# Graph attention on one core: segment maxima by scans over 32 steps at once

## The chip, the cores and the metric

One of the eight cores of a Trainium2 chip runs one program. The metric is the device time in microseconds (us); the kernel before takes 11579.1 us, the median of three runs.

## The reference

Four graph layers over 12,500 nodes of 128 features, each followed by a residual and a layer norm. The edges, 200,000 of them, are sorted by their target `dst`. Layer 0 averages neighbours, layer 1 mixes the 16 neighbours of a ring, layer 2 is graph attention, layer 3 is two graph convolutions. The change is in layer 2:

```
hs = h[src]
a  = hs @ Ws.T + h[dst] @ Wd.T + emb_rel[etype] @ Wr.T
e  = leaky_relu((a @ attn_fc2_w.T)[:, 0], 0.01)        # one logit an edge
m  = segment_max(e, dst);  w = exp(e - m[dst])
denom = segment_sum(w, dst);  alpha = w / denom[dst]
agg = segment_sum(alpha[:, None] * hs, dst)
agg = where(deg > 0, agg, h);  out = agg + h @ loop_weight
```

## The kernel before

Nodes stand in 98 tiles of 128. The sorted edges are cut into 1660 steps (`STEPS`) of up to 128 edges, so that the targets of one step lie in one node tile; an edge is a partition, a step a column of `src_idx` and `dst_local` (the target's place in its tile). Three layers walk over the steps in turn. In the attention stage every step j does this:

- GpSimd gathers 128 rows of 132 words (128 features, a one, the source's part of the logit, two coefficients) from `attention_rows` in HBM by an indirect DMA (L1987) into one of 28 row slots; a slot is free when the product of step j-28 is done (`a_summed`) and its group of 7 steps is drawn (`a_coefs`).
- VectorE builds a one-hot [edge, node] in bf16 (L2052, `edges_hot`); TensorE turns it (L2095), ScalarE copies it out of PSUM (L2120, `nodes_hot`), and TensorE multiplies it by three bf16 pieces of the target's scores (L2087). Every 7 steps `draw_vector` (L2002 to L2011) makes the logits.
- VectorE masks the logits into a [edge, node] matrix (L2043), TensorE turns it (L2080), VectorE takes the maximum over the edges for each node (L2037) and then the minimum with the node's running negative maximum (L2033). ScalarE makes the factor for the old sum (L2113), keeps the maximum (L2116) and takes the exponentials of the whole matrix (L2108). TensorE turns the weights back (L2073), ScalarE copies them (L2104), TensorE multiplies by the gathered rows (L2069, two passes in float32), and VectorE scales the accumulator and adds (L2025). Each `added` waits for the one before.

Steps are staggered by hand: every engine walks over the same list of moments (`steps_due`, 28 hops) and does, in a fixed order, what is due for different steps. Two matmuls a step (`keep_warm`, L2059) have no reader. Each VectorE, ScalarE and TensorE part that addresses a node tile reads its column from registers, loaded eight steps at a time.

Before the stage: `attention_gpsimd` begins when the dense product of layer 1 is done. SyncE reloads step data and then loads `loop_rows` (6.4 MB, L1923) into `x_all` for the layer's end. After it: `finish3` walks over the 98 tiles on VectorE (divide by the denominator, add the loop row L2167, add own rows of nodes with no edge L2161, statistics and norm); SyncE loads own rows through an 8-slot ring (L2176). Then the convolution stage follows.

## Time and profile before

| | |
|---|---|
| median of 3 runs (lowest, highest) | 11579.1 us (11574.55, 11604.76) |
| span of the profiled execution, first to last instruction | 9485.5 us |
| time of the profiled execution outside its span | not reported by the profile |
| median less span | 2093.6 us |
| instructions in the trace | 179289 |
| mean granted TensorE clock (1.0 is full speed) | 0.865 |

Of an engine the profile gives busy time (the union of its instructions) and idle time ahead of each group of instructions, with the instruction of another engine whose semaphore ended it ("<- PE banks L2069"); "issue" is a wait for which the profile shows no releaser. Instructions of one engine overlap at their ends, so that the mean durations of a step's instructions add up to more than the busy time.

### The profile page before, as it was taken

To read this page: it belongs to the slowest core of one execution; us is meant where nothing else is said; L and a number is where in the kernel's file an instruction comes from. 1 tells how busy PE (TensorE), PEld (TensorE's weight loads), DVE (VectorE), ACT (ScalarE), POOL (GpSimd) and SP (SyncE) were. 2 spreads that over 40 slices of the span, in tenths; PEclk is the share of its full clock that TensorE was granted. 3 is DMA by queue.
4 is the path that set the end of the run, shared out by engine and by line. 5 is a ranking of instruction groups with operands and counts; after the bars stand their busy time and mean duration, and the time that the engine had idled before them with its cause. 6 is when DMAs were issued, how large, how long until landed. Compare 5 with 4: busy or idle time off the path is not lost.

```text
span 9485.5 us, 179289 instructions
## 1 busy us (share of the span) xinstructions
PE 7300.6 (77%) x42403; PEld 5513.2 (58%) x42403; DVE 7417.6 (78%) x24801; ACT 6576.3 (69%) x18731; POOL 6416.0 (68%) x6972
## 2 busy tenths in 40 slices
PE   4444444555689999999989999788888888838887
PEld 3333444444467777788878787555555555525555
DVE  7766666666788999566667777788888888899899
ACT  6777777777877777111178866577777777758885
POOL 0377777777347777777677777666666666639894
PEclk8555555555799999999999999999999999979997
DMA  3222222222477777888877752322222222210001
GB/s 55 50 53 53 53 53 52 53 52 53 125 257 258 254 260 257 317 327 318 292 267 257 254 191 67 84 51 50 50 51 50 50 51 50 50 36 1 1 2 28
DMA packets 499507, 1146.68 MB, mean 121 GB/s; under 512 B 149534, under 2 KB 352994, under 8 KB 478894
## 3 DMA queue, kind: packets, MB, share of 16 engines
q0 software_dynamic: 212688, 491.92, 19.3%
q10 hardware_dynamic: 21888, 497.76, 13.5%
q1 hardware_dynamic: 263902, 145.55, 5.7%
q8 instruction: 369, 6.05, 0.3%
q14 instruction: 660, 5.41, 0.2%
HBM read 888.41 MB, written 252.74 MB: 120 GB/s over the span
## 4 chain that ended last, share of the span: by engine, by line
PE 27%; DVE 27%; issue 17%; ACT 14%; POOL 7%; DVEq 4%; DMA 2%; SPq 1%; ACTq 0%; POOLq 0%
PE banks L1423 17%; POOL step_data L1765 7%; ACT banks L1185 3%; DVE step_small L2037 3%; DVE keys L2043 3%; PE banks L1049 2%; PE banks L1409 2%; DVE keys L1109 2%; ACT onehot L1038 2%; DVE gather_ring L2243 2%; DVE keys L1118 2%; ACT onehot L1036 2%; DVEq L1065 2%; DVE arena L2253 2%; DVE arena L2025 2%
## 5 line engine op out<-in xcount | busy, mean ns | idle before, releaser
L1024 POOL DMA_INDIRECT gather_ring<-mean_rows,step_data x1660 | 1597.4, 962 | 744.2 <-issue 322.4
L1049 PE MATMUL banks<-gather_ring,onehot 128*128 128x130 f32 x3320 | 950.9, 449 | 1127.4 <-DVE arena L1082 949.0
L1423 PE MATMUL banks<-arena 128*128 128x384 bf16 x8232 | 1549.0, 327 | 30.5 <-DMA arena<-split_out 26.5
L1049 PEld LDWEIGHTS banks<-gather_ring,onehot 128*128 128x128 f32 x3320 | 792.5, 301 | 1280.1 <-issue 1047.2
L1423 PE MATMUL banks<-arena,keys 128*128 128x384 bf16 x8134 | 1529.0, 327 | 3.9 <-DMA arena<-split_im 3.9
L1423 PEld LDWEIGHTS banks<-arena 128*128 128x128 bf16 x8232 | 1133.8, 138 | 263.2 <-issue 31.2
L1423 PEld LDWEIGHTS banks<-arena,keys 128*128 128x128 bf16 x8134 | 1119.8, 138 | 232.9 <-issue 5.0
L1765 POOL DMA_INDIRECT step_data<-next_rows,window_idx x992 | 945.3, 953 | 347.8 <-issue 300.2
L1456 POOL DMA_INDIRECT step_data<-hidden,window_idx x924 | 897.7, 972 | 323.2 <-issue 267.0
L1987 POOL DMA_INDIRECT gather_ring<-attention_rows,step_data x834 | 788.3, 945 | 392.9 <-PE banks L2069 218.5
L1987 POOL DMA_INDIRECT keys<-attention_rows,step_data x826 | 779.5, 944 | 367.7 <-PE banks L2069 254.8
L2059 PE MATMUL banks<-iota_quad,ident_half 128*128 128x256 bf16 x3320 | 913.5, 275 | 104.4 <-DVE arena L2025 86.1
L1036 ACT ACTIVATE onehot<-iota_row,step_data 128x128 f32<-128x128 f32 x1660 | 644.4, 388 | 436.4 <-PE banks L1049 410.7
L2226 POOL TENSOR_SCALAR onehot<-iota_row,step_data,window_idx 128x128 f32<-128x128 f32 x996 | 777.6, 792 | 84.6 <-PE banks L2291 63.3
L1082 DVE TENSOR_TENSOR arena<-arena,banks 128x130 f32 x1660 | 482.0, 290 | 402.7 <-DVE arena L1082 229.2
L2025 DVE SCALAR_TENSOR_TENSOR arena<-arena,step_small,banks 128x129 f32 x1660 | 581.8, 351 | 226.3 <-ACT step_small L2113 84.3
L2113 ACT ACTIVATE step_small<-arena,step_small 128x1 f32 x1660 | 489.3, 295 | 350.2 <-DVE step_small L2033 321.3
L1456 POOL DMA_INDIRECT gather_ring<-hidden,window_idx x612 | 591.9, 967 | 207.0 <-issue 177.5
L1038 ACT ACTIVATE onehot<-onehot,ones 128x128 f32<-128x128 f32 x1660 | 666.4, 401 | 53.8
L1415 ACT ACTIVATE arena<-banks 128x392 bf16<-128x392 f32 x1088 | 519.9, 501 | 196.0 <-PE banks L1409 143.3
L2080 PE MATMUL banks<-ident,keys 128*128 128x128 f32 x1660 | 539.6, 325 | 144.4 <-DVE keys L2043 53.5
L1415 ACT ACTIVATE keys<-banks 128x392 bf16<-128x392 f32 x1056 | 506.7, 498 | 199.9 <-PE banks L1409 147.0
(324 smaller groups left out, 19507.1 us busy)
## 6 DMA issues: line engine op xcount, KB each, us to landing
keys<-count_rows ACTq DMA_DIRECT2D x48, 3136.0 KB
arena<-count_rows ACTq DMA_DIRECT2D x48, 3136.0 KB
count_rows<-arena ACTq DMA_DIRECT2D x25, 3136.0 KB
count_rows<-keys ACTq DMA_DIRECT2D x25, 3136.0 KB
gather_ring<-mean_rows,step_data POOLq DMA_INDIRECT x1660
step_data<-next_rows,window_idx POOLq DMA_INDIRECT x992
step_data<-hidden,window_idx POOLq DMA_INDIRECT x924
gather_ring<-attention_rows,step_data POOLq DMA_INDIRECT x834
```

Of the source, the lines that this page charges most:

```text
L1024: e.indirect_dma_start(ring_at(rings.slot(name, i), SUM_COLS, SUMS - 1), None, rows, bass.IndirectOffsetOnAxis(src_idx[:, i:i + 1], 0), bo ...
L1036: e.activation(h, iota_row[:, :], ACT.Abs, bias=dst_local[:, j:j + 1], scale=-1.0).then_inc(hot_made)
L1038: e.activation(h, h, ACT.Relu, bias=ones[:, 0:1], scale=-1.0).then_inc(hot_made)
L1049: e.matmul(pass_bank[i % N_SUM_BANKS][:, 0:SUMS], onehot[:, i % STEP_SLOTS, :], ring_at(rings.slot(name, i), SUM_COLS, SUMS), start=True, ...
L1415: e.activation(counts[t % 2][:, 4 * g:4 * g + 4, :], count_bank[b % len(count_bank)][:, 0:GROUP_COLS].rearrange("p (q h) -> p q h", q=4), ...
L1423: m = e.matmul(pass_bank[n % 2][:, 0:SPLIT_COLS], counts[t % 2][:, :, h], split[:, h, :], start=(h == 0), stop=(h == NODE_TILES - 1))
L1456: e.indirect_dma_start(first_rows(i)[:, a, :], None, hidden1, bass.IndirectOffsetOnAxis(gather_idx[:, at:at + 1], 0), bounds_check=None).t ...
L1765: e.indirect_dma_start(batch_rows[:, i % BATCH_SLOTS, r, :], None, next_rows, bass.IndirectOffsetOnAxis(gather_idx[:, at:at + 1], 0), boun ...
L1987: e.indirect_dma_start(attention_row(j), None, attention_rows, bass.IndirectOffsetOnAxis(src_idx[:, j:j + 1], 0), bounds_check=None).then_inc(
L2025: e.scalar_tensor_tensor(part, part, step_small[:, s, 3:4], step_sums(j), ALU.mult, ALU.add).then_inc(a_added)
L2059: e.matmul(bank[:, 0:WARM_COLS], ident_half[:, :], warm_row, start=True, stop=True)
L2226: e.tensor_scalar(onehot[:, p % CONV_HOTS, :], iota_row[:, :], dst_local[:, j:j + 1], edge_norm[:, j:j + 1], ALU.is_equal, ALU.mult).then_ ...
```

## The change

A step no longer holds a masked matrix and per-node maxima. Since edges are sorted by target, a node's edges are a contiguous run, within a step or over several. For a span of 32 steps at once (52 spans, the last of 28 steps) the logits [128 edges, 32 steps] are turned to [32 steps, 128 edges]; a forward and a backward scan that add -2^100 at each change of target and take maxima (`local_vector`), a scan over the 32 ends (`cross_vector`, on one partition) and two scans with the carried-in maxima (`final_vector`) give each edge its segment's maximum. One Exp makes all 32 x 128 weights; one node a span, that which began in the span before, has its sum rescaled. A step then keeps: one weighted one-hot (float32, VectorE), one product, one addition. The bf16 one-hots of the logits are made four steps in one instruction, turned by plain matmuls, and copied four at once. `keep_warm` is gone. The rows ring has 96 slots, in the arena, where `x_all` was filled with loop rows; `finish3` now loads loop rows tile by tile, beside the own rows. `flags_vector` makes the flags of continued segments from a new load (`last_target`) before the first step. Span work of the coming span is placed at fixed distances (`left`) before the end of the running span.

```diff
-HOT_SLOTS = 2 * STEP_SLOTS
+SPAN, SPAN_SLOTS, HOT_BATCH = 32, 3, 4
+SPANS = -(-STEPS // SPAN)
+SPAN_SIZES = [min(SPAN, STEPS - g * SPAN) for g in range(SPANS)]
...
-        for s in range(FEW_SLOTS):
-            e.wait_ge(loop_stored[s], 16 * len(range(s, NODE_TILES, FEW_SLOTS)))
-        e.dma_start(x_all.rearrange("p (t d) -> p t d", d=D),
-                    loop_rows.rearrange("(t p) d -> p t d", p=P)).then_inc(x_loaded, 16)
+        e.dma_start(last_target, step_rows[P - 1:P, STEP_COLS:2 * STEP_COLS]).then_inc(steps_back, 16)
...
+    def moments():
+        for g in range(-1, SPANS):
+            first, n = (0, SPAN) if g < 0 else span_of(g)
+            for i in range(n):
+                yield g, g + 1 if g + 1 < SPANS else None, i, i - n, first + i if g >= 0 else None
+    def batch_due(p, i, hop):
+        b, odd = divmod(i - hop, 2)
+        return b if p is not None and not odd and 0 <= b < SPAN_SIZES[p] // HOT_BATCH else None
...
-                e.wait_ge(a_summed, j - ATTENTION_SLOTS + 1)
-                e.wait_ge(a_coefs, 2 * ((j - ATTENTION_SLOTS) // DRAWN + 1))
-            e.indirect_dma_start(attention_row(j), None, attention_rows,
+            if j >= ROW_SLOTS:
+                if j % SPAN == 0:
+                    e.wait_ge(a_coefs, 2 * ((j - ROW_SLOTS) // SPAN + 1))
+                e.wait_ge(a_summed, j - ROW_SLOTS + 1)
+            e.indirect_dma_start(row_ring[:, j % ROW_SLOTS, :], None, attention_rows,
                                  bass.IndirectOffsetOnAxis(src_idx[:, j:j + 1], 0),
-                                 bounds_check=None).then_inc(
-                rings.landed("attention", j // DRAWN)[0], 16)
...
+    def flags_vector(e):
...
+        e.wait_ge(steps_back, 64)
+        e.tensor_copy(target_half[:, :], dst_local).then_inc(a_flags)
...
+        e.tensor_tensor(broken_whole, first, last_target, ALU.not_equal).then_inc(a_flags)
+        e.wait_ge(a_flags, 3)
+        e.tensor_tensor(flag_room[:, 1:], flag_room[:, 1:], last_target[:, :-1], ALU.subtract).then_inc(a_flags)
...
+    def logits_vector(e, p):
...
+        rows = row_ring[:, first % ROW_SLOTS:first % ROW_SLOTS + n, :]
+        l, done, cols = logit[:, p % 2, 0:n], DRAW_STEPS * p, slice(first, first + n)
+        e.wait_ge(a_score, batches_before(p + 1))
+        if p >= 2:
+            e.wait_ge(a_tensor, SCALES * (p - 2) + LOGITS)
+        e.tensor_reduce(l, span_scores(p, n), AX.X, ALU.add).then_inc(a_logit)
+        e.wait_ge(*rings.landed("attention", p))
+        e.tensor_copy(edge_norm[:, cols], rows[:, :, D + 3]).then_inc(a_coefs)
...
+    def local_vector(e, p):
+        n = SPAN_SIZES[p]
+        e.wait_ge(a_scalar, SCALE_KEPT * p + RESET)
+        e.wait_ge(a_tensor, SCALES * p + LOGITS)
+        e.tensor_tensor_scan(forward[0:n, 0:P], reset[0:n, 0:P], span_logits[0:n, :], -MASK, ALU.add,
+                             ALU.max).then_inc(a_vector)
+        e.tensor_tensor_scan(backward[0:n, P - 1::-1], reset[0:n, P:0:-1], span_logits[0:n, ::-1], -MASK, ALU.add,
+                             ALU.max).then_inc(a_vector)
+    def cross_vector(e, p):
+        first, n = span_of(p)
+        heads = head_rows[n < SPAN]
+        e.wait_ge(a_tensor, SCALES * p + TAILS)
...
+    def final_vector(e, p):
+        first, n = span_of(p)
+        done = ROW * p + CROSSED
+        e.wait_ge(a_tensor, SCALES * p + CARRIES)
+        e.tensor_copy(carry_kept[0:n, :], span_carry[0:n, :]).then_inc(a_vector)
...
+        e.tensor_tensor_scan(carried[0:n, 0:P], reset[0:n, 0:P], span_logits[0:n, :], carry_kept[0:n, 0:1], ALU.add,
+                             ALU.max).then_inc(a_vector)
+        e.wait_ge(a_vector, done + 2)
+        e.tensor_tensor_scan(highest[0:n, P - 1::-1], reset[0:n, P:0:-1], carried[0:n, P - 1::-1],
+                             carry_kept[0:n, 1:2], ALU.add, ALU.max).then_inc(a_vector)
+        e.wait_ge(a_vector, done + 3)
+        if p:
+            e.wait_ge(a_tensor, SCALES * (p - 1) + BACK)
...
+    def weighted_vector(e, j):
+        g = j // SPAN
+        if j >= STEP_SLOTS:
+            e.wait_ge(a_summed, j - STEP_SLOTS + 1)
+        e.wait_ge(a_scalar, SCALE_KEPT * g + WEIGHT)
+        e.tensor_scalar(onehot[:, j % STEP_SLOTS, :], iota_half[:, :], dst_local[:, j:j + 1],
+                        weight[:, g % SPAN_SLOTS, j % SPAN:j % SPAN + 1], ALU.is_equal, ALU.mult).then_inc(a_weighted)
+    def added_vector(e, j, late_regs):
+        g, i = divmod(j, SPAN)
+        if j:
+            e.wait_ge(a_added, j)
+        if i == 0:
+            part, = late_regs.parts(e, j, (0, D + 1))
+            e.wait_ge(a_scalar, SCALE_KEPT * g + SCALE_KEPT)
+            e.scalar_tensor_tensor(part, part, scale_kept, part, ALU.mult, ALU.add).then_inc(a_scaled)
+            e.wait_ge(a_scaled, g + 1)
+        part, = late_regs.parts(e, j, (0, D + 1))
+        e.wait_ge(a_summed, j + 1)
+        e.tensor_tensor(part, part, sum_bank[j % SUM_SLOTS], ALU.add).then_inc(a_added)
...
+        flags_vector(e)
+        for g, p, i, left, j in moments():
+            if (b := batch_due(p, i, 0)) is not None:
+                k, at = batches_before(p) + b, p * SPAN + b * HOT_BATCH
+                if k >= HOT_BUFS:
+                    e.wait_ge(a_turned, k - HOT_BUFS + 1)
+                e.tensor_tensor(
+                    edges_hot[:, k % HOT_BUFS, :, :],
+                    target_half[:, at:at + HOT_BATCH].rearrange("p (o c) -> p o c", o=1).to_broadcast([P, P, HOT_BATCH]),
+                    iota_quad[:, :, :], ALU.is_equal).then_inc(a_hot)
+            if p is not None:
+                if left == -14:
+                    e.wait_ge(a_scalar, SCALE_KEPT * p + TARGETS_KEPT)
+                    if p:
+                        e.wait_ge(a_scalar, SCALE_KEPT * (p - 1) + RESET)
+                    n = SPAN_SIZES[p]
+                    e.tensor_tensor(change[0:n, 0:P - 1], targets[0:n, 0:P - 1], targets[0:n, 1:P],
+                                    ALU.not_equal).then_inc(a_vector)
+                if left == -12:
+                    logits_vector(e, p)
+                if left == -10:
+                    local_vector(e, p)
+                if left == -8:
+                    cross_vector(e, p)
+                if left == -6:
+                    final_vector(e, p)
+                if left == -4:
+                    rescale_vector(e, p)
+                if left >= -WEIGHT_AHEAD:
+                    weighted_vector(e, p * SPAN + WEIGHT_AHEAD + left)
+            if j is not None:
+                if left < -WEIGHT_AHEAD:
+                    weighted_vector(e, j + WEIGHT_AHEAD)
                 if j:
-                    e.wait_ge(a_added, j)
-                e.scalar_tensor_tensor(part, part, step_small[:, s, 3:4], step_sums(j), ALU.mult,
-                                       ALU.add).then_inc(a_added)
...
+        for g, p, i, left, j in moments():
+            if (b := batch_due(p, i, 3)) is not None:
+                k, n = batches_before(p) + b, SPAN_SIZES[p]
+                e.wait_ge(a_nodes, k + 1)
+                if p >= 2 and b == 0:
+                    e.wait_ge(a_logit, DRAW_STEPS * (p - 2) + 1)
...
+                    m = e.matmul(span_scores(p, n)[:, step, :], nodes_hot[:, k % HOT_BUFS, c * P:(c + 1) * P], parts,
+                                 start=True, stop=True)
+                m.then_inc(a_score)
+            if (b := batch_due(p, i, 1)) is not None:
+                k = batches_before(p) + b
+                if k >= TURN_BUFS:
...
+                first, n = span_of(p)
+                if left == -16:
+                    if p:
+                        e.wait_ge(a_scalar, SCALE_KEPT * (p - 1) + TARGETS_KEPT)
+                    e.transpose(span_targets[0:n, :], dst_local[:, first:first + n], ident[:, :]).then_inc(a_tensor)
...
+                    e.transpose(span_scale, rescale_row, ident[0:1, 0:1]).then_inc(a_tensor)
+            if j is not None:
+                if j >= SUM_SLOTS:
+                    e.wait_ge(a_added, j - SUM_SLOTS + 1)
+                e.wait_ge(a_weighted, j + 1)
+                e.matmul(sum_bank[j % SUM_SLOTS], onehot[:, j % STEP_SLOTS, :], row_ring[:, j % ROW_SLOTS, 0:D + 1],
+                         start=True, stop=True).then_inc(a_summed)
...
+        for g, p, i, left, j in moments():
+            if (b := batch_due(p, i, 2)) is not None:
+                k = batches_before(p) + b
+                e.wait_ge(a_turned, k + 1)
+                if k >= HOT_BUFS:
+                    e.wait_ge(a_score, k - HOT_BUFS + 1)
+                e.activation(nodes_hot[:, k % HOT_BUFS, :], turn_bank[k % TURN_BUFS], ACT.Copy).then_inc(a_nodes)
+            if p is not None:
...
+                if left == -4:
+                    if p >= SPAN_SLOTS:
+                        e.wait_ge(a_weighted, (p - SPAN_SLOTS + 1) * SPAN)
+                    e.wait_ge(a_tensor, SCALES * p + BACK)
+                    e.activation(weight[:, p % SPAN_SLOTS, 0:n], span_back[:, 0:n], ACT.Exp).then_inc(a_scalar)
...
+            e.dma_start(loop_many[:, t % 8, :], loop_rows[tile_rows(t), :]).then_inc(piece_stored[t % 8], 16)
...
-        e.wait_ge(a_kept, STEPS)
```

## Rows read from the trace of the kernel before

**Rows 1.** Windows: length, busy (count) of PE, PEld, DVE, ACT, POOL, clock, DMA share, GB/s.

```profile
374.00:2482.00 2108.00, 1006.74 (x3832) 853.73 (x3832) 1393.35 (x2344) 1588.12 (x3637) 1592.84 (x1659) 0.56 0.25 56
2482.00:6022.00 3540.00, 3362.54 (x19959) 2706.89 (x19959) 2719.56 (x7730) 2063.90 (x4013) 2435.40 (x2530) 0.98 0.70 248
6032.00:8371.00 2339.00, 1902.57 (x13280) 1234.26 (x13280) 1997.19 (x9738) 1829.33 (x8302) 1567.68 (x1660) 0.98 0.23 53
8371.00:8493.00 122.00, 1.27 (x3) 0.68 (x3) 116.88 (x584) 29.23 (x100) 19.85 (x98) 0.50 0.22 53
```

**Rows 2.** Line L1987, the gathers: min/median/max ns, first and last start.

```profile
L1987 POOL DMA_INDIRECT gather_ring<-attention_rows,step_data x834: 938/944/1007, 6031.9 to 8333.4; - x167
...
```

**Rows 3.** Timeline of GpSimd at the stage's start: start, us, [idle before].

```profile
6031.88 0.94 POOL L1987 DMA_INDIRECT gather_ring<-attention_rows,step_data  x1 [25.89 <-DMA step_data<-step_rows]
...
6101.86 0.94 POOL L1987 DMA_INDIRECT gather_ring<-attention_rows,step_data  x1 [0.30 <-PE banks L2069]
```

**Rows 4.** Waits from 6200 to 8300 us: total, times, longest.

```profile
POOL keys L1987 <- PE banks L2069: 237.2, 459, 1.8
POOL gather_ring L1987 <- PE banks L2069: 205.9, 362, 1.9
...
DVE step_small L2033 <- issue: 65.3, 201, 0.8
```

**Rows 5.** Groups from 6200 to 8300 us (1507 steps): count, busy, mean ns.

```profile
L2025 DVE SCALAR_TENSOR_TENSOR arena<-arena,step_small,banks 128x129 f32 x1507 | 528.2, 350 | 205.2 <-ACT step_small L2113 77.4 <-PE banks L2069 52.5 <-issue 21.6
L2043 DVE TENSOR_SCALAR keys<-keys,small 128x128 f32<-128x128 bf16 x1506 | 481.8, 320 | 0.0
L2037 DVE TENSOR_REDUCE step_small<-banks 128x1 f32<-128x128 f32 x1506 | 428.9, 285 | 0.4
L2052 DVE TENSOR_SCALAR keys<-iota_half,step_data 128x128 bf16<-128x128 bf16 x1507 | 410.2, 272 | 5.7 <-issue 5.4 <-PE banks L2087 0.3
L2033 DVE TENSOR_TENSOR step_small<-arena,step_small 128x1 f32<-128x1 f32 x1506 | 249.0, 165 | 78.8 <-issue 65.3 <-ACT arena L2116 11.8
```

**Rows 6.** Lines elsewhere: min/median/max ns, or idle us and times, or busy, mean ns.

```profile
L1396 DVE TENSOR_TENSOR onehot<-arena,iota_quad x536: 384/424/477, 2694.9 to 5994.3; 128x512 bf16<-128x512 bf16 x179
L1082 DVE TENSOR_TENSOR arena<-arena,banks x1660: 271/291/459, 383.5 to 2482.2; 128x130 f32 x185
...
  DVE arena L1082: 229.2, 1102
...
L1117 DVE TENSOR_TENSOR keys<-keys,banks x174: 1212/1220/2042, 404.2 to 2101.3; 128x1024 f32<-128x1024 f32 x174
L1415 ACT ACTIVATE keys<-banks 128x392 bf16<-128x392 f32 x1056 | 506.7, 498 | 199.9 <-PE banks L1409 147.0
```

**Rows 7.** Timeline of the mean stage at half clock, and L2187's one transpose.

```profile
1502.30 3.72 PE L1049 MATMUL banks<-gather_ring,onehot 128*128 128x130 f32 x14 [5.56 <-DVE arena L1082]
L2187 PE MATMUL banks<-ident,arena x1: 474/474/474, 8378.4 to 8378.4; 128*128 128x128 f32 x1
```

**Rows 8.** Groups of the dense stage, 2482 to 4700 us: its gathers.

```profile
L1456 POOL DMA_INDIRECT step_data<-hidden,window_idx x918 | 892.0, 972 | 321.4 <-issue 265.2 <-DVE banks L1470 33.0 <-DVE banks L1465 23.2
```

**Rows 9.** Timeline of VectorE around the stage's two ends.

```profile
6032.52 10.95 DVE L1933 MEMSET arena<- 128x13068 f32 x1 [2.86 <-issue]
6045.18 0.38 DVE L1944 CAST arena<-inv_deg 128x98 bf16<-128x98 f32 x1
...
6053.09 0.18 DVE L2002 TENSOR_REDUCE small<-banks 128x7 f32<-128x21 f32 x1 [6.09 <-PE banks L2087]
...
8370.23 0.35 DVE L2025 SCALAR_TENSOR_TENSOR arena<-arena,step_small,banks 128x129 f32 x1 [0.23 <-PE banks L2069]
...
8371.05 0.77 DVE L2144 RECIPROCAL keys<-keys 128x98 f32<-128x98 f32 x1
```

**Rows 10.** SyncE's queue: two issues in a row, late in the dense stage.

```profile
6029.49 0.32 SPq L1910 DMA_DIRECT2D attention_rows<-wide_few  x1
6029.85 0.43 SPq L1912 DMA_DIRECT2D loop_rows<-turned_few  x1
```

More of the change, by code:

```diff
@@ L417, in program @@
                              ("second", BATCH_SLOTS, [BATCH] * SECOND * BATCHES),
-                             ("attention", ATTENTION_SLOTS // DRAWN,
-                              [min(DRAWN, STEPS - g * DRAWN) for g in range(DRAWS)])))
+                             ("attention", SPAN_SLOTS, SPAN_SIZES)))
     ring_ones = sem("ring_ones_set")
@@ L1958, in program @@
[L1958 to L1977 removed]
+    ACC_READY = 6
@@ new lines, in program @@
+    logit = attention_room[:, room_at:room_at + 2 * SPAN].rearrange("p (b s) -> p b s", b=2)
+    room_at += 2 * SPAN
+    weight = attention_room[:, room_at:room_at + SPAN_SLOTS * SPAN].rearrange("p (b s) -> p b s", b=SPAN_SLOTS)
+    room_at += SPAN_SLOTS * SPAN
+    reset, change, targets, forward, backward, carried, highest, below_max = (
+        attention_room[0:SPAN, room_at + i * (P + 2):room_at + (i + 1) * (P + 2)] for i in range(8))
+    room_at += 8 * (P + 2)
+    carry_kept, scale_kept = attention_room[0:SPAN, room_at:room_at + 2], attention_room[:, room_at + 2:room_at + 3]
@@ new lines, in program @@
+    carry_row = attention_room[0:1, room_at + 4:room_at + 4 + 2 * SPAN]
+    room_at += 4 + 2 * SPAN
+    head_rows = [attention_room[0:1, room_at + i * (SPAN + 1):room_at + (i + 1) * (SPAN + 1)] for i in range(2)]
+    room_at += 2 * (SPAN + 1)
+    rescale_row, rescale = attention_room[0:1, room_at:room_at + P], attention_room[0:1, room_at + P:room_at + P + 3]
+    running = keys_all[0:1, STEP_COLS:2 * STEP_COLS + 1]
+    flag_room = keys_all[0:1, STEP_COLS:2 * STEP_COLS]
+    last_target = gather_ring[0:1, 0:STEP_COLS]
@@ new lines, in program @@
+    TARGETS, LOGITS, TAILS, CARRIES, BACK, SCALES = 1, 2, 3, 4, 5, 6
+    turn_bank = [bank_all[i] for i in range(TURN_BUFS)]
+    score_bank, span_bank = bank_all[2], bank_all[3]
+    sum_bank = [bank_all[4 + i][:, 0:D + 1] for i in range(SUM_SLOTS)]
+    span_targets, span_logits = span_bank[0:SPAN, 0:P], span_bank[0:SPAN, P:2 * P]
+    span_tails = [span_bank[0:1, (2 * P + i * SPAN):2 * P + (i + 1) * SPAN] for i in range(2)]
+    span_carry = span_bank[0:SPAN, 2 * P + 2 * SPAN:2 * P + 2 * SPAN + 2]
@@ new lines, in program, with span_of, span_scores, batches_before @@
+    span_back = span_bank[:, 2 * P + 3 * SPAN:2 * P + 4 * SPAN]
+    span_scale = span_bank[:, 3 * P:3 * P + 1]
+    def span_of(g):
+        first = g * SPAN
+        return first, SPAN_SIZES[g]
+    def span_scores(g, n):
+        at = (g % 2) * SPAN * PIECES
+        return score_bank[:, at:at + PIECES * n].rearrange("p (s k) -> p s k", k=PIECES)
+    def batches_before(g):
+        return sum(n // HOT_BATCH for n in SPAN_SIZES[:g])
+    def moments():
[3 more added lines that the diff above has]
+                yield g, g + 1 if g + 1 < SPANS else None, i, i - n, first + i if g >= 0 else None
@@ L2005, in draw_vector @@
         e.wait_ge(a_logit, done + 1)
-        e.tensor_tensor(l, l, edge_score[:, first:end], ALU.add).then_inc(a_logit)
+        e.tensor_tensor(l, l, edge_score[:, cols], ALU.add).then_inc(a_logit)
         e.wait_ge(a_logit, done + 2)
         e.tensor_tensor(l, l, rows[:, :, D + 1], ALU.add).then_inc(a_logit)
-        e.tensor_copy(edge_coef[:, first:end], rows[:, :, D + 2]).then_inc(a_coefs)
+        e.tensor_copy(edge_coef[:, cols], rows[:, :, D + 2]).then_inc(a_coefs)
         e.wait_ge(a_logit, done + 3)
@@ new lines, in rescale_vector @@
+    def rescale_vector(e, p):
+        first, _ = span_of(p)
+        e.wait_ge(a_scalar, SCALE_KEPT * p + ALPHA)
+        e.tensor_scalar(rescale[:, 2:3], rescale[:, 2:3], -1.0, None, ALU.add).then_inc(a_vector)
+        e.wait_ge(a_vector, ROW * p + FINAL + 1)
+        if p:
+            e.wait_ge(a_tensor, SCALES * (p - 1) + SCALES)
+        e.tensor_scalar(rescale_row, iota_row[0:1, :], dst_local[0:1, first:first + 1], rescale[:, 2:3], ALU.is_equal,
+                        ALU.mult).then_inc(a_vector)
@@ L2172, in finish3_sync @@
         wait_stored(e, STORES2, 4)
+        for s in range(FEW_SLOTS):
+            e.wait_ge(loop_stored[s], 16 * len(range(s, NODE_TILES, FEW_SLOTS)))
         for t in range(NODE_TILES):
```

312 lines of the change are left out of this document (148 added, 164 removed).

## The prediction, made before the changed kernel was run

> **What bounds the kernel now.** I read the windows by stage first [rows 1]: the attention stage takes 2339 of the 9485.5 us of the span, from the first gather at 6031.9 to the last addition at 8370.6. The stages before it and the convolution after it keep their code, so the question is what this stage becomes. No engine is full in it: VectorE is busy 1997 of 2339 us (85%), TensorE 1903, ScalarE 1829, GpSimd 1568. Next the gathers [rows 2]: 1660 of them start between 6031.9 and 8333.4 us, so 2301.5 / 1659 = 1.387 us from one to the next. The timeline of GpSimd [rows 3] shows what a gather costs if nothing holds it: 0.94 us, then 0.30 us of "issue"; the reader is to see that the 57th gather (6101.86) stands 69.98 us after the first, so that one follows the other in 69.98 / 56 = 1.250 us. That is the floor of the queue of gathers, and the stage lies only 0.137 us a step above it. The waits [rows 4] tell what makes up the rest: GpSimd waits 443 us in 2100 for products (L2069) to free row slots, that is, for the other engines. The groups of VectorE [rows 5] tell why that is slow: five operations a step of 0.350, 0.320, 0.285, 0.272 and 0.165 us, and six small ones every seven steps (0.18 us as L2002 [rows 9], 0.15 us a step): 1.54 us a step if added, 1997 / 1660 = 1.20 in busy time (they overlap at their ends), in one order with TensorE's three turns and ScalarE's four large operations, whose hops wait for each other (VectorE's L2025 77 us for ScalarE, 53 for TensorE). The loop through VectorE, TensorE and ScalarE sets 1.387; the gathers come close behind.
>
> **The gathers after.** The change removes none: 1660 rows of 128, same table, same queue. The wait for a free slot stays, one a step; 96 slots in place of 28 and a wait for `a_coefs` every 32 steps only loosen it. Hence the least stage is 1659 x 1.250 = 2073.8 us from first to last gather, against 2301.5: 227.7 us less. That is all that can be had here, however little is left for the other engines.
>
> Is 1.250 the right price? The upper end is the dense stage's gathers: 0.972 us [rows 8] and the same 0.30 us, 1.272, which would give back 0.022 x 1659 = 37 us. That stage moves 248 GB/s, this one 53 [rows 1], and 1.250 is the mean here over one memset of VectorE (6032.5 to 6043.5) and over its full work (6053 on) [rows 9]. I take 1.250.
>
> **VectorE after.** A step: the weighted one-hot (bf16 in, float32 out, two scalars of which one was a constant in L2043: 0.320 [rows 5]), the addition (L1082's form, 0.291 [rows 6]), and a quarter of a four-step one-hot (L1396's very form, 0.424 / 4 = 0.106): 0.717 us, where five operations and the draw were 1.54. A span has 22 more operations (one for the changes, six for logits, two scans, four and six in `cross` and `final`, two and one for the rescale). Some twelve are small, 0.18 each as L2002 [rows 9]: 2.2. Four of 128 columns as L1082: 1.2. The trace has no scan. Below, one costs no less than an addition of its length, 0.291; above, I take the reciprocal of 98 columns, 0.77 [rows 9], three times an ordinary operation of that width. Four long at 0.4 and two short at 0.25 make 2.1 (1.7 to 4.6 at the ends). I choose nearer the lower row, because a scan is one add and one maximum an element. Sum 5.5. Each dependent operation waits for the one ahead (0.20 us in L1082, 229.2 / 1102 [rows 6]), twelve times: 2.4. The chain changes engine five times in a span (logits, tails, carries, back, scale), each time two moments apart, with a moment of VectorE's own work (0.7 us) to cover a transpose of 0.474 at half clock [rows 7]; I put 0.5 each, 2.5. Register loads: 65.3 / 201 = 0.32 us if they are what "issue" stands for in front of L2033 [rows 4], five a span: 1.6. A span thus needs 32 x 0.717 + 5.5 + 2.4 + 2.5 + 1.6 = 34.9 us with full durations, 37.4 with dear scans. The gathers need 32 x 1.250 = 40.0. VectorE waits for rows, at `logits_vector`. What queues behind that wait are the additions and one-hots of the last 12 steps of the span before; they are late by the wait, and no gather waits for them: at that moment 44 to 64 rows are in hand, of 96 slots.
>
> A sentence apart on the scans: the Trainium skill (DVE: opcode table, instruction layouts, handler registers and perf-mode slots, section "Datapath and trigger behaviour") says that `tensor_tensor_scan` runs at half throughput. Doubling the length-dependent part of an addition's 0.291 gives an estimate of some 0.42 us, and no row here shows one.
>
> **TensorE and ScalarE after.** Both lose most. TensorE keeps two float32 passes a step, a turn, a product of three columns, and six transposes a span. Without `keep_warm` (3320 matmuls) and two of three turns it is busy under half the time; in the mean stage, at 1007 of 2108 us busy, it was granted 0.56 [rows 1], so I expect the lower of its two levels, 1.2 GHz, in most of the stage. Two passes cost 3.72 / 7 = 0.53 us there [rows 7]; with the small ones 0.8 a step, below 1.250. It costs nothing while the gathers bind. ScalarE: 512 columns every four steps, about 0.6 as L1415's 0.498 for 392 [rows 6], 0.15 a step.
>
> **Start.** VectorE reaches `flags_vector` at about 6045.6 [rows 9]. Ten rows of 1664 elements at L1117's pace, 1.22 x 1664 / 1024 = 2.0 us [rows 6], end at about 6066; eight four-step one-hots through the turns take some 7 us more: 6073. The 32nd gather starts at 6070.6. Both meet, and nothing in GpSimd waits: its 97th gather (6151.9) needs the product of step 0, due near 6090. The flags' 20 us are hidden under the first 32 gathers; without that cover they would cost 20. The load of `loop_rows`, at the head of the stage, goes away; gathers were issued at their floor beside it [rows 3], so nothing is gained.
>
> **End.** Before, 36.8 us pass from the last gather to the last addition [rows 2, 9]. After: about 3 us to land and draw, twelve moments with the chain (8.6 + 10.4), 28 steps of 0.717 (20.1): 42 with full durations, 33 if they overlap as before (1.20 / 1.54). I take +2. In `finish3`, 122 us for 98 tiles [rows 1] is VectorE's, 1.24 a tile; SyncE now issues two loads a tile, 0.32 + 0.43 = 0.75 us [rows 10], below 1.24 and eight tiles ahead. Its first addition, which found its row in `x_all`, now waits for a load: one operation of the pipeline is exposed, +1 with its issue. If SyncE needed over 1.24 a tile, each 0.1 above would cost 10.
>
> **Sum.** -227.7 + 2 + 1 = -225 us on the span: 9485.5 to 9260.5. The profile gives no time of its execution outside the span; the median is 2093.6 us above it, of which no view shows anything. I carry that over unchanged: 11579.1 - 225 = 11354.
>
> **Rivals.**
> *VectorE binds partly.* It does from 40.0 us a span, 5.1 above my sum; a hop of 1.5 instead of 0.5 us would do. At 42 the stage is 52 x 2 = 104 us longer: about 11458. For it: dependent chains on one in-order engine. Against: full durations already overstate (1.54 against 1.2). 12%, 2 of them so far that it comes within 0.3% of the old time.
> *VectorE makes it slower.* The same chain past 44.4 us a span (32 x 1.387), 9.5 over my sum: six scans of 1.6 us more than I gave each. At 48 it gives 52 x 8 = 416 more than 11354: 11770. No row near a scan is above 0.77. 4%.
> *Gathers held by VectorE.* If the weighted one-hot held back the gather beside it for its 0.320 us, a gather would take 1.570, 1659 of them 2605 us: 303 more than before, 11882. It turns slower from 0.137 a gather. Before, two such operations ran in every step (L2043, L2052 [rows 5]), and the median gather was 0.944 with 1.007 us at most [rows 2]. 3%. The Trainium skill's rule for this is in SBUF — State Buffer, section "SBUF: two separate sides": while VectorE runs in a two-port mode GpSimd cannot write descriptors. By that rule, the trace's gathers should be longer beside those operations, and they aren't.
> *What lies around the span shrinks.* The stage's instructions [rows 1] fall: TensorE's by 2 x 6300 (four matmuls a step less, six a span more), VectorE's by 4850, ScalarE's by 7600: 25,000, 14% of the 179289. If the 2093.6 us followed that, 293 us more would go: 11061. Nothing speaks for it but its size. 7%.
> *As forecast*, 11330 to 11400: 74%.
>
> **Numbers.** The runs of before differ by 0.26%; 0.3% (35 us) is about what tells a change of this kernel from none. Faster 74 + 10 + 7 = 91%, less a little for what I don't see: 0.89; within 0.3% 0.04; slower 0.07. The range has the forecast with gathers at up to 1.272 (11391) and most of the first rival (to 11480); below, a shorter end: 11310.
>
> **What would show it.** Right: gathers 1.250 apart from first to last, GpSimd's idle all "issue", VectorE's wait in front of the logits' copy ended by the rows' DMA, clock near 0.5. Wrong: waits of GpSimd for products or `a_coefs`; scans above 1.5 us; gathers of over 1.0 us; a median that doesn't follow the span.

## The result, and the profile after

| | before | after |
|---|---|---|
| time in the comparison, median (us) | 11588.3 (11574.6 to 11604.8) | 11398.0 (11392.3 to 11424.4) |
| ratio, 95% interval | | 0.984 (0.982 to 0.986) |
| profiled execution (us) | span 9485.5 | span 11399.8, time 11401.6 |

The forecast was 11354 in 11310 to 11480, and faster at 0.89: it is faster, by 190 us where 225 were forecast. (Of the 44 us between forecast and median 9 are the kernel before, at 11588.3 instead of 11579.1.) The last line of the table is odd. After the change nothing but 1.8 us lies outside the span, where my sum carried 2093.6.

The windows by stage of the profiled execution after the change, columns as in [rows 1]:

```profile
370.00:2849.00 2479.00, 1028.76 (x3833) 875.19 (x3833) 1395.63 (x2365) 1607.07 (x3638) 1599.60 (x1660) 0.56 0.21 48
2849.00:7740.00 4891.00, 3840.61 (x19979) 2726.93 (x19979) 2708.96 (x7739) 2042.57 (x4015) 2430.00 (x2530) 0.88 0.52 179
7740.00:10282.00 2542.00, 1369.95 (x7056) 1113.48 (x7056) 1274.47 (x4904) 303.93 (x677) 1606.16 (x1660) 0.51 0.20 45
10282.00:10407.00 125.00, 1.27 (x3) 0.68 (x3) 117.90 (x587) 29.16 (x100) 20.21 (x99) 0.50 0.40 103
```

The mean stage and the dense stage, whose code did not change, take 2479 and 4891 us in place of 2108 and 3540 [rows 1]. The attention does what the diff says (VectorE's busy time 1997 to 1274 us, ScalarE's 1829 to 304), and yet its 2542 us are more than the 2339 of [rows 1]. Against that trace alone one would call the change slower. The gathers' line, as in [rows 2]:

```profile
L2017 POOL DMA_INDIRECT arena<-attention_rows,step_data x1660: 942/947/2335, 7742.6 to 10197.6; - x185
```

2455.0 / 1659 = 1.480 us from one gather to the next, not 1.250. The waits from 7900 to 9700 us (total, times, longest), where [rows 4] had 443 us of GpSimd for products:

```profile
ACT keys L2266 <- remote: 588.1, 105, 9.5
...
DVE arena L2152 <- PE banks L2254: 350.2, 299, 3.0
DVE arena L2152 <- remote: 345.8, 147, 5.0
PE banks L2206 <- ACT keys L2266: 324.4, 82, 6.6
...
POOL arena L2017 <- remote: 209.5, 139, 2.5
POOL arena L2017 <- PE banks L2254: 156.2, 220, 2.6
```

"Remote" is a release whose sender the profile does not find. Three engines have it in front of exactly the operations that wait for TensorE.

### The profile page after: what moved, and what is told of

Its sections match the earlier page's. It is cut to its first block, busy times and chain, and to the rows that moved or that the text cites. A ratio compares the mean times of both kernels' runs of the same rounds, so it can differ in the third digit from the quotient of the medians.

```text
span 11399.8 us, 142237 instructions
## 1 busy us (share of the span) xinstructions
PE 7265.4 (64%) x36179; PEld 5433.9 (48%) x36179; DVE 6681.4 (59%) x19966; ACT 5047.7 (44%) x11106; POOL 6455.1 (57%) x6972
## 4 chain that ended last, share of the span: by engine, by line
PE 29%; another core or an unknown queue 15%; issue 14%; DVE 12%; ACT 5%; DVEq 1%; DMA 1%; SPq 1%; POOL 0%; ACTq 0%; POOLq 0%
PE banks L1413 16%; PE banks L1399 4%; PE banks L2254 3%; DVE gather_ring L2418 2%; PE banks L2206 1%; PE banks L2215 1%; DVE arena L2428 1%; DVE banks L1714 1%; PE banks L2466 1%; ACT keys L1728 1%; ACT keys L1726 1%; DVEq L1055 1%; ACT keys L2266 1%; DVE banks L1458 0%
## 5 line engine op out<-in xcount | busy, mean ns | idle before, releaser
L2017 POOL DMA_INDIRECT arena<-attention_rows,step_data x1660 | 1606.2, 968 | 893.3 <-issue 367.8
L1413 PE MATMUL banks<-arena 128*128 128x384 bf16 x8232 | 1735.7, 349 | 192.0 <-issue 167.9
L1413 PE MATMUL banks<-arena,keys 128*128 128x384 bf16 x8134 | 1709.9, 347 | 195.3 <-issue 189.9
L2152 DVE TENSOR_TENSOR arena<-arena,banks 128x129 f32 x1660 | 479.2, 289 | 1057.1 <-PE banks L2254 467.6
L2254 PE MATMUL banks<-arena,onehot 128*128 128x129 f32 x3320 | 954.4, 444 | 13.9 <-DVE arena L2152 11.7
L2266 ACT ACTIVATE keys<-banks 128x512 bf16<-128x512 f32 x415 | 247.8, 597 | 1376.7 <-remote 790.6
L2254 PEld LDWEIGHTS banks<-arena,onehot 128*128 128x128 f32 x3320 | 781.9, 325 | 35.1 <-DVE arena L2152 19.2
L1399 PE MATMUL banks<-keys,onehot 128*128 128x392 bf16 x1600 | 560.1, 352 | 260.7 <-issue 140.4
```

Source lines behind the costliest of these rows:

```text
L1399: e.matmul(count_bank[b % len(count_bank)][:, 0:GROUP_COLS], low_hot[c % 2][:, :, i], high_hot[b >= ROUND][c % 2][:, i, :], start=True, st ...
L1413: m = e.matmul(pass_bank[n % 2][:, 0:SPLIT_COLS], counts[t % 2][:, :, h], split[:, h, :], start=(h == 0), stop=(h == NODE_TILES - 1))
L2017: e.indirect_dma_start(row_ring[:, j % ROW_SLOTS, :], None, attention_rows, bass.IndirectOffsetOnAxis(src_idx[:, j:j + 1], 0), bounds_chec ...
L2254: e.matmul(sum_bank[j % SUM_SLOTS], onehot[:, j % STEP_SLOTS, :], row_ring[:, j % ROW_SLOTS, 0:D + 1], start=True, stop=True).then_inc(a_s ...
```

## The experiments

Two questions were open: why do the two profiled executions differ by 1900 us, and what holds the gathers at 1.48? In all, the kernel before was timed in five comparisons. In two it took 11588 and 11432 us, in three 9491, 9492 and 9491. I call these condition B and condition A. Medians are compared within one condition only; in B the kernel before itself differs by 1.4% between the two comparisons, so there a ratio holds within one comparison. No run shows what sets the condition. The experiments in B (e1 to e3) ran on chip 15, those in A on chips 2, 14 and 13; of the first comparison the chip isn't recorded. That fits a property of the chip and doesn't show it: no kernel was timed on one chip in both conditions.

**e1_before_again: the kernel before, once more** (no edit).

> The kernel before, unchanged. Its trace spans 9485.5 us though its three timed executions took 11575 to 11605 us; the changed kernel's trace spans 11399.8 us for an execution of 11401.6, and in it the mean stage takes 2479 us (2108 in the trace of before), the dense stage 4891 (3540), the attention stage 2520 (2339) and the convolution the same 943. Theory A (the trace of before is of an execution under other conditions than the timed ones; both kernels suffer alike where they gather): this trace spans about 11590, mean stage about 2480, dense about 4890, convolution 943, and the attention stage about 2520 + 190 = 2710 us, that is 1.6 us a step. Theory B (the changed kernel itself slows the stages ahead of the attention, whose code is the same): mean and dense stage stay at 2108 and 3540 here and about 2090 us lie outside the span.

Its profiled execution took 11475.9 us, its span 11474.2. Theory A holds: nothing lies outside the span. The trace ahead of the prediction is simply of an execution in condition A, and the times shown beside it are of condition B. Its windows by stage:

```profile
370.00:2835.00 2465.00, 1018.63 (x3832) 866.93 (x3832) 1394.52 (x2360) 1606.07 (x3638) 1599.59 (x1660) 0.56 0.22 48
2835.00:7678.00 4843.00, 3816.57 (x19980) 2729.11 (x19980) 2715.56 (x7746) 2048.85 (x4015) 2425.16 (x2530) 0.88 0.53 181
7678.00:10360.00 2682.00, 2081.62 (x13280) 1414.26 (x13280) 2005.37 (x9734) 1861.76 (x8302) 1569.46 (x1660) 0.89 0.21 46
```

VectorE's busy time hardly differs from [rows 1]: its operations are as long as ever. What grows is the waiting, in the three stages that gather, and the dense stage moves 181 GB/s in place of 248. (This one execution is 44 us longer than the median of the same kernel in its comparison, 11432.1, so the differences to it below carry some tens of microseconds.) In condition B the attention before takes 2682 us; that is what 2542 and 2515 (below) stand against.

**e2_base: the change, with one wait moved.** TensorE enters the attention after the last small load. This kernel is the basis of all that follow.

```diff
     def attention_tensor(e, regs):
         e.wait_ge(score_steps, ACC_READY)
-        e.wait_ge(steps_back, 48)
+        e.wait_ge(steps_back, 64)
```

> The changed kernel; TensorE's first wait for the step data is for all four loads and not for three, nothing else. Both theories: ratio to before 0.984, span within 3 us of the time; gathers 1.48 us apart.

11272.1 us against 11432.1 (ratio 0.985, 0.983 to 0.988): 160 us less, a gain whose interval overlaps that of the change itself. Span by span against the kernel before again, 11474.2 to 11286.3: the attention starts 23.9 us earlier (the code ahead of it is the same in both), its gathers take 2430.9 in place of 2644.4 (-213.5), 83.3 us in place of 37.6 pass from the last gather to the last addition (+45.7), and the rest takes 1117.7 in place of 1113.8 (+3.9). The timeline shows what the gathers stand behind:

```profile
8298.60 1.23 PE L2254 MATMUL banks<-arena,onehot 128*128 128x129 f32 x4
...
8301.53 0.17 ACT L2292 ACTIVATE keys<-banks 128x1 f32<-128x1 f32 x1 [3.98 <-remote]
8301.53 0.29 DVE L2152 TENSOR_TENSOR arena<-arena,banks 128x129 f32 x1 [3.11 <-remote]
8301.67 0.95 POOL L2017 DMA_INDIRECT arena<-attention_rows,step_data  x1 [2.11 <-remote]
...
8307.37 0.59 PE L2215 MATMUL banks<-ident_half,keys 128*128 128x128 bf16 x4 [0.86 <-issue]
...
8311.66 0.60 ACT L2266 ACTIVATE keys<-banks 128x512 bf16<-128x512 f32 x1 [6.56 <-remote]
```

Four passes of TensorE are recorded as over at 8299.83; ScalarE, VectorE and GpSimd are let go together at 8301.5 to 8301.7. The turned one-hots are done at 8307.96, and their copy starts 3.7 us later. (Ends of matmuls are modelled in these records; whether the product or its message is late can't be told.)

**e3_warm: TensorE kept warm.** The change drops `keep_warm`; here it is back.

```diff
+                for _ in range(4):
+                    keep_warm(e, turn_bank[k % TURN_BUFS])
...
+                keep_warm(e, bank_all[4 + j % SUM_SLOTS])
```

> The changed kernel with matmuls that nobody reads put back on TensorE in the attention stage, two a step of 256 columns as before. In the changed kernel's trace TensorE is granted 0.51 there, the two passes of a step cost 445 ns each. Theory W (the half clock lengthens the chain VectorE, TensorE, VectorE and so the stage): clock about 0.98, passes near 305 ns, and the stage falls from 2520 by 100 us or more. Rival R (the stage is held by moments in which several engines stand still at once with no releaser in the profile, whatever TensorE's clock): the stage stays within 30 us of 2520, and is longer if more instructions make more such moments.

11359.3 us (ratio 0.994, 0.992 to 0.996), 87 slower than without. In the attention's window the granted clock was 0.76 in place of 0.51, a product's pass 0.335 us in place of 0.447 in the mean, and the stage still grew from 2514.2 to 2574.6 us. Theory W fails as stated, but its 0.98 was not reached, and the run adds work to TensorE along with the clock; it doesn't price the clock alone. That the half clock is not what makes B slow is shown by e8 below: the same kernel was granted 0.53 in A and its stage took 2140 us.

**e4_no_refill: nothing gathered after the first 96 steps.** (This and the next three ran in condition A, together.)

```diff
             if j >= ROW_SLOTS:
-                if j % SPAN == 0:
-                    e.wait_ge(a_coefs, 2 * ((j - ROW_SLOTS) // SPAN + 1))
-                e.wait_ge(a_summed, j - ROW_SLOTS + 1)
+                continue
...
-        e.wait_ge(*rings.landed("attention", p))
+        e.wait_ge(*rings.landed("attention", p % SPAN_SLOTS))
```

> The changed kernel (with TensorE's first wait of the attention at the last load, as in e2_base) in which GpSimd gathers only the first 96 rows' worth of steps and then stops: later steps read what lies in the 96 slots. Everything that the other engines do is left as it is. In e2_base the attention took 2514.2 us from its first gather to its last addition, 1.515 us a step, and the gathers ran 90 to 92 steps ahead, against the ring's end. Theory P (the ring is always full, the other engines' own chain sets the pace, and the gathers' floor of 1.250 us is not reached): the attention stays above 1.35 us a step, 2240 us or more, and the time falls by less than 200 us against e2_base's 11272. Theory G (the gathers' transfers are what makes the other engines' chain slow, through late semaphores or memory): it falls under 1.2 us a step, to below 2000 us, and the time below 10780.

8868.0 us; the attention's window:

```profile
6033.00:7750.00 1717.00, 1331.20 (x7056) 1093.33 (x7056) 1239.58 (x4902) 303.73 (x677) 99.02 (x96) 0.54 0.02 5
```

1716.3 / 1659 = 1.035 us a step: all that VectorE, TensorE and ScalarE need for a step in condition A, 33.1 us a span. By the bounds set ahead that is Theory G's side, but those were set against condition B's 1.515 and the run fell into A: it says that the gathers bind in A, and nothing of why B is slow.

**e5_extra_vector: more work for VectorE.**

```diff
+                if left < -WEIGHT_AHEAD:
+                    e.wait_ge(a_spare, spare_steps.setdefault(j, len(spare_steps)))
+                    e.tensor_scalar(spare, iota_half[:, :], dst_local[:, j:j + 1], weight[:, g % SPAN_SLOTS, i:i + 1],
+                                    ALU.is_equal, ALU.mult).then_inc(a_spare)
```

> e2_base with one more 128x128 one-hot (about 0.35 us) on VectorE in 29 of 32 steps, written to a place that nobody reads: 1500 x 0.353 = 530 us more work for VectorE. Theory P as I hold it (VectorE has room, it was busy 1.26 ms of 2.5; what sets the pace are TensorE's two passes at half clock, 2 x 0.447 us a step, and the waits between engines): under 150 us more than e2_base. Theory V (VectorE's order of work sets the pace; every instruction on it adds its length): 400 to 530 us more.

9320.4 us, 25.8 more than the same kernel without it (9294.6, in the comparison of e8 below; the kernel before took 9491.5 and 9492.3 in the two), though VectorE was busy 342 us longer in the stage (1605). In A VectorE has room.

**e6_hops: later hops.** ScalarE's copy three steps after the one-hots, TensorE's score products five.

```diff
-            if (b := batch_due(p, i, 3)) is not None:
+            if (b := batch_due(p, i, 5)) is not None:
...
-            if (b := batch_due(p, i, 2)) is not None:
+            if (b := batch_due(p, i, 3)) is not None:
```

> e2_base with two of the hops of a batch of four steps later: ScalarE's copy of the turned one-hots three steps after VectorE made them (before: two), TensorE's score products five after (before: three), so that each has one step more between it and what it waits for. In e2_base TensorE's score products L2206 waited 310 us for ScalarE's copy and 186 without a named cause. Theory P1 (TensorE standing in its order for the copy is part of the pace): 60 to 300 us faster than e2_base. Rival P2 (TensorE gets the same waits one instruction later, at the spans' chain or the product): within 40 us of it.

9290.5 us: in condition A no gain to be seen against 9294.6.

**e7_product_half: half the columns of the product.**

```diff
-                e.matmul(sum_bank[j % SUM_SLOTS], onehot[:, j % STEP_SLOTS, :], row_ring[:, j % ROW_SLOTS, 0:D + 1],
+                e.matmul(sum_bank[j % SUM_SLOTS][:, 0:D // 2 + 1], onehot[:, j % STEP_SLOTS, :], row_ring[:, j % ROW_SLOTS, 0:D // 2 + 1],
```

> e2_base whose step products cover 65 of the 129 columns (the rest of the sums is not made; VectorE still adds all 129). The two passes of a product took 0.447 us each at the half clock; with half the columns about 0.25 to 0.3 us, so 0.3 to 0.4 us a step less for TensorE. Theory P (TensorE's work at the half clock is part of every step's pace): 200 to 600 us faster than e2_base. Theory L (latency between the engines alone, TensorE's load beside it): under 100 us faster.

9293.5 us, no gain. Nor did a pass get much shorter, where 0.25 to 0.3 us was expected: 0.420 us for 65 columns, 0.443 for 129 (means, lines 6300 to 8000 us). Between 65 and 129 columns a float32 pass hardly depends on them here. The bounds of e5, e6 and e7 were set against B's kernel, whose pace they were to explain; in A, where the gathers bind, none of the three says anything of it.

**e8, e9, e10: the basis, without refills, and hops, in one comparison** (kernels of e2, e4 and e6).

> e2_base once more, as the partner of the two that follow. On the chip of e2_base the kernel before took 11432 us and this one 11272; in the comparison of e4 to e7 the kernel before took 9491, its attention's gathers were then at 1.27 us a step in e5 to e7, close to their floor, and the trace that the prediction used was of that sort (9486 us). Theory T (two conditions of the chip, the forecast's floor holds in the quicker one only): if the kernel before takes about 9490 here, this one takes 9285 to 9330 with 2100 to 2125 us from its first to its last gather; if it takes about 11430, this one takes 11250 to 11300, 2400 to 2450 us of gathers. Rival S (the gathers at 1.27 in e6 and e7 came from what these two changed): at 9490 this one takes 9340 or more and its gathers over 2150 us.

> e4 once more (only the first 96 gathers are made): where the kernel before takes about 9490 it was 1.035 us a step. Where it takes about 11430, Theory G2 (what makes the other engines' chain slow there is tied to the gathers' transfers in flight): 1.0 to 1.15 us a step, the attention's 2514 us of e2_base falls to 1700 to 1900. Theory P2 (the chain itself is slow there, whether anything is gathered or not): 1.35 us a step or more, 2240 us or more.

> e6 once more, beside e2_base's kernel on the same chip. Where the kernel before takes about 9490 the gathers are at their floor and it is within 20 us of e8_base_again. Where it takes about 11430 the waits for ScalarE's copy are part of the pace: 40 to 300 us faster than e8_base_again; rival: within 40 us there too, since the late releases then hit the next wait in TensorE's order.

Condition A again: 9294.6, 8872.3 and 9288.8 us beside 9492.3. For the change that is a ratio of 0.979 (0.977 to 0.981), 197.7 us less. Theory T holds, S falls. G2, P2 and the question of the hops in B got no answer. The basis' windows of attention and `finish3`, and its gathers' line:

```profile
6038.00:8178.00 2140.00, 1350.28 (x7056) 1110.72 (x7056) 1262.56 (x4901) 303.88 (x677) 1603.38 (x1660) 0.53 0.25 54
8178.00:8303.00 125.00, 1.27 (x3) 0.69 (x3) 118.06 (x589) 29.30 (x101) 20.66 (x99) 0.51 0.41 103
```

```profile
L2017 POOL DMA_INDIRECT arena<-attention_rows,step_data x1660: 940/944/2328, 6037.9 to 8146.0; - x185
```

2108.1 / 1659 = 1.271 us. Its waits from 6200 to 8000 us:

```profile
ACT keys L2266 <- PE banks L2215: 657.3, 348, 3.0
...
DVE window_idx L2061 <- DMA arena<-attention_rows,step_data: 385.0, 45, 9.4
DVE arena L2152 <- PE banks L2254: 283.4, 335, 1.9
POOL arena L2017 <- issue: 280.0, 919, 0.3
POOL arena L2017 <- PE banks L2254: 153.0, 502, 0.3
```

No "remote" is left, GpSimd never waits over 0.3 us, and VectorE stands 8.6 us a span (385.0 / 45) at the logits for rows to land. Slower transfers do not explain B either. The gathers' queue in the attention's window, here and in e2 (packets, MB, share of the 16 engines' time; windows 6038 to 8178 us here, 7654 to 10169 us in e2, that is 2140 and 2515 us):

```profile
q0 software_dynamic: 53120, 112.30, 24.2%
q0 software_dynamic: 53120, 112.30, 20.6%
```

24.2% of 2140 and 20.6% of 2515 are both 518 us: the packets take as long in B as in A. The groups of VectorE in the same stretch, as in [rows 5]:

```profile
L2137 DVE TENSOR_SCALAR onehot<-iota_half,step_data,keys 128x128 f32<-128x128 bf16 x1416 | 513.0, 363 | 1.4 <-PE banks L2254 0.9 <-issue 0.2
L2152 DVE TENSOR_TENSOR arena<-arena,banks 128x129 f32 x1416 | 406.5, 287 | 322.6 <-PE banks L2254 283.4 <-issue 32.5 <-DVE arena L2148 5.9
L2163 DVE TENSOR_TENSOR keys<-edge_type,iota_quad 128x512 bf16<-128x512 bf16 x352 | 147.5, 419 | 0.2
L2107 DVE TENSOR_TENSOR_SCAN keys<-keys 32x128 f32<-32x128 f32 x45 | 23.4, 521 | 1.6
...
L2075 DVE TENSOR_TENSOR_SCAN keys<-keys,banks 32x128 f32<-32x128 f32 x45 | 18.0, 401 | 0.2 <-issue 0.2
L2077 DVE TENSOR_TENSOR_SCAN keys<-keys,banks 32x128 f32<-32x128 f32 x45 | 17.2, 382 | 0.0
...
L2085 DVE TENSOR_TENSOR_SCAN keys<-few_all,keys,banks 1x32 f32<-1x32 f32 x45 | 11.8, 262 | 0.0
...
L2087 DVE TENSOR_TENSOR_SCAN keys<-few_all,banks 1x32 f32<-1x32 bf16 x45 | 8.2, 182 | 0.0
```

What is left above 1.250 is in the gathers' own length. The timelines of GpSimd and of VectorE at the stage's start:

```profile
6051.68 1.78 POOL L2017 DMA_INDIRECT arena<-attention_rows,step_data  x1 [0.30 <-issue]
...
6059.27 1.50 POOL L2017 DMA_INDIRECT arena<-attention_rows,step_data  x1 [0.30 <-issue]
```

```profile
6051.61 1.03 DVE L2025 CAST edge_type<-step_data 128x1664 bf16<-128x1664 f32 x1
...
6058.07 1.87 DVE L2032 TENSOR_TENSOR keys<-keys,gather_ring 1x1663 f32<-1x1663 f32 x1
```

The gather of 6051.68 ends at 6053.46, 0.82 us after L2025's end at 6052.64; that of 6059.27 at 6060.77, 0.83 us after L2032's end at 6059.94. Each looks as if it had stood still from shortly after its start until the operation beside it was over. Beside the flags' wide rows eight gathers in a row take 1.49 to 2.33 us. Over the stage 193 of 1660 take more than 1.0 us, against 2 before, and the mean is 0.966 in place of 0.9445: 35 us in all, 6 of them at the flags. The same sign is on the short ones. Take the gathers at whose start an operation of VectorE was already running, with more than 0.2 us to go: beside L2163 88 of 90 took over 1.0 us, and all 88 ended 0.81 to 0.82 us after the operation; beside L2148 (two inputs in SBUF too) 30 of 34; beside the addition L2152, one of whose inputs is in PSUM, none of 105; beside the weighted one-hot L2137 6 of 214. In the trace before none of 137 took over 1.0 us beside L2052 and none of 28 beside L2043 (its two long ones, with 0.2 us to go or less, ended 0.82 us after an L2043). Of the 706 gathers that started with VectorE idle none took over 1.0 us. With the extra one-hot of VectorE it was 0.976, 17.4 us more, which is two thirds of what that kernel lost; another 6 us are its tail after the last gather.

**e11, e12: without refills a third time, and 64 row slots.**

```diff
-SPAN, SPAN_SLOTS, HOT_BATCH = 32, 3, 4
+SPAN, SPAN_SLOTS, HOT_BATCH = 32, 2, 4
```

> The kernel of e4 and e9 (only the first 96 gathers are made), in the hope of a chip on which the kernel before takes about 11430. There: Theory G2 (what slows the other engines' chain is tied to the gathers' transfers): 1.0 to 1.15 us a step, and ScalarE's copy L2264 starts as promptly after its product as in e8. Theory P2 (late releases come without gathers too): 1.35 us a step or more. Where the kernel before takes about 9490: 1.036 us a step again, 8870 us.

> e2_base's kernel with 64 row slots and two of weights in place of 96 and three. Theory R1: where the kernel before takes about 9490, the gathers ran 36 to 42 steps ahead of the weighted one-hots, under 64, so the ring is still long enough: 9280 to 9310, gathers 2100 to 2130. Rival R2: a ring that must hold one span in use and one landing stands full at times (GpSimd waits for the products): gathers over 2200 us, 9380 or more. Where the kernel before takes about 11430, the ring is always full, its depth only decides how many steps are left after the last gather: 30 us less after the last gather (83 in e2_base), and as much more before it, so within 40 us of e2_base's ratio of 0.9853.

Condition A once more: 8869.2 and 9292.9 us. R1 holds, the stage takes 2136.5 us with 64 slots and 2139.7 with 96. (Counted from the starts, from step 200 on, the gathers ran 34 to 42 steps ahead of the weighted one-hots in A, and 87 to 92 in B, near the ring's end of 96.) The cause of the late releases in B stayed out of reach. No version beat the change by more than the measurement tells.

## Why the forecast came out right in sign and 44 us low

In the comparison on record the number is near by luck. Three of the prediction's own signs of being wrong are in its profile: GpSimd waits for products, 143 of 1660 gathers take over 1.0 us, and the median doesn't follow the span of the trace that was used. Its mechanism, the gathers' floor, holds in condition A.

- **The gathers' floor: the main step, right in condition A.** Forecast 2073.8 us, measured 2108.1 there, -193.4 against [rows 2] in place of -227.7. The missing 34 us are the longer gathers (35). In B, where the recorded comparison ran, the floor is not reached at all: the gathers stand at the products, and their gain of 213.5 comes from the shorter chain of the other engines. That the two gains are alike is chance. (213.5 is the difference of two single executions.)
- **Which price of a gather.** I took the median of a stage where gathers were long in 2 of 1660 cases and dismissed the rival of gathers held by VectorE, because L2043 and L2052 did not lengthen them. Gathers are held by VectorE, but hardly by the operation that the rival named (6 of 214 beside the weighted one-hot), and for far less than its price: 0.021 us a gather in the mean, not 0.320. Most of it comes from new operations: the flags' rows, and L2163 and L2148, whose two inputs lie in SBUF. The Trainium skill (SBUF — State Buffer, section "SBUF: two separate sides") names two cases, an operation of VectorE in a two-port mode, or one with two inputs from SBUF against a GpSimd operation that reads SBUF, and calls the port pair an exclusive lock; I had weighed only its first case. A gather reads its indices from `step_data` in SBUF. The trace agrees for L2163 (88 of 90 held, 0.81 to 0.82 us from its end to the gather's) and for the addition with an input in PSUM (none of 105), but not for every such operation: beside the scan L2107, with two inputs in SBUF, 3 of 38 took over 1.0 us. That a lock is the reason is the page's statement.
- **VectorE's budget: right.** 34.9 us a span were forecast; the whole loop without gathers needs 33.1, and VectorE's wait for rows is 8.6 us a span where 40.0 less 34.9 leaves 5.1. The weighted one-hot costs 0.363 (0.320 forecast), the addition 0.287 (0.291), long scans 0.38 to 0.52 (0.4), short ones 0.18 and 0.26 (0.25). TensorE was granted 0.53 in the stage, the lower of its levels for most of it, and that cost nothing in A, as forecast.
- **Start: the flags were hidden, but not free:** they ended at 6066.8 us (6066 forecast) and lengthened the gathers beside them by 6 us. That the two times agree is chance: the rows took 15 us where 20 were forecast, and the stage began 6 us later (6037.9 against 6031.9). The code ahead of it is unchanged, and in the other runs of condition A the first gather starts between 6027.9 and 6038.5, so these 6 us are scatter.
- **The end.** `finish3` costs 2 us more (125 against 122.9), +1 forecast. From last gather to the start of the last addition it is 31.7 us in A (39 forecast, 36.8 before): full durations overstated it. In B it is +45.7, the step that failed there. I had argued it from the last span's 28 steps; a ring of 96 that stands full leaves some 90 steps to do, at 0.9 us each (83.3 us in all). A deeper ring moves time from the gathers to behind them.
- **"Carried over unchanged": wrong as a picture, harmless as a number.** I took the median's 2093.6 us over the span for something outside it. It was inside: the trace was of condition A. The sum came near only because both kernels lose alike from A to B (1940 us before, 1977 after), which nothing in the prediction had a reason for. The rival that this surplus shrinks with the instructions falls with it.
- **Added up in A:** start +6.0, gathers -193.4, tail -5.1, rest +2.0, together -190.5: 9485.5 to 9294.9, against -225. In the recorded comparison -190.4, which came about in another way: a longer tail, and the wait for products in place of the floor.

Still open: what makes releases of TensorE 2 to 5 us late in B. By e8 neither TensorE's clock nor the time that the packets take does it. For it being tied to the gathers speaks only that the stages which gather nothing take the same time in both, the convolution 991 to 993 us and `finish3` 123 to 125. It isn't shown: no run without gathers fell in B.

## What to carry to other kernels

Before a sum is made against a trace, compare its span with the time of its own execution and with the median: a gap of a fifth is a question about the trace's conditions, not a constant to carry over. Where a queue has a floor, price it by its mean beside the new neighbours, not by the median beside the old ones. The largest gain that a floor allows says nothing of a run in which the ring stands full: read there who waits with the ring at its end, and count the steps that are left behind it.

## What the runs showed of the hardware

- A gather's issue on GpSimd (0.944 us) lasts up to 2.33 us beside VectorE operations on 1664 elements, and over 1.0 us in 184 other cases of 1660 in e8. Beside a `tensor_tensor` of 128x512 in bf16 with both inputs in SBUF that was already running and had over 0.2 us to go, 88 of 90 ended 0.81 to 0.82 us after that operation; beside an addition with one input in PSUM none of 105 took over 1.0 us.
- In one condition of the chip, releases from TensorE came microseconds late to three engines at one moment, and every stage that gathers took 15 to 38% longer, with operations of the same length and 518 us of gather packets a DMA engine in both conditions.
- A scan of 32x128 cost 0.38 to 0.52 us on VectorE where an addition of 128x129 costs 0.287.
- Four extra matmuls a batch and one a step raised the granted clock from 0.51 to 0.76 and made the stage 60 us longer.
